# Sixteen heads' values, the state's share and the sums of squares in one block of column tiles per chunk

## What is computed

```
xn = layernorm(x)
q, k, v = silu(xn Wq'), silu(xn Wk'), xn Wv'      lf = cumsum of log_sigmoid(xn Wf' + delta) in the chunk
for each chunk, per head:
    A = (q k') * exp(lf_i - lf_j) for j <= i
    o = A v + (q exp(lf)) S
    S = exp(tot) S + (k exp(tot - lf))' v
s = (o * rsqrt(mean(o*o) + 1e-6) * norm_weight) Wo'
out = x + s * silu(experts(xn))
```

## Time and profile before

| | us |
|---|---|
| median of 3 runs | 893.77 |
| lowest and highest of them | 892.22 and 895.04 |
| the profiled execution's own time | 893.34 |
| its span in the profile | 891.6 |

### The profile page before, as it was taken

How to read it: one execution, slowest core, us unless ns; L and a number is a source line. 1 busy time by engine, 2 the same in 40 slices (tenths; PEclk the granted TensorE clock), 3 DMA queues, 4 the chain that set the end, 5 groups by cost and what they waited for, 6 DMA issues and landing times.

```text
span 891.6 us, 15824 instructions
## 1 busy us (share of the span) xinstructions
PE 800.4 (90%) x5648; PEld 682.0 (76%) x5648; DVE 566.5 (64%) x1027; ACT 498.7 (56%) x1165; POOL 429.0 (48%) x383
## 2 busy tenths in 40 slices
PE   1665799999999999999999999999999999999930
PEld 1443578888888888888888888888888888888830
DVE  5685455657855775557665766568656766556575
ACT  4654755566546664665556645665566545654431
POOL 5647641656245642566255815563357525470230
PEclk9965699999999999999999999999999999999975
DMA  8756796658667775678576766676667767663947
GB/s 284 283 166 157 206 343 221 159 152 186 194 157 159 188 195 143 150 183 202 154 160 181 156 219 142 164 187 193 157 140 193 195 157 210 162 134 117 277 106 221
DMA packets 132847, 163.89 MB, mean 184 GB/s; under 512 B 11808, under 2 KB 102432, under 8 KB 132640
## 3 DMA queue, kind: packets, MB, share of 16 engines
q1 hardware_dynamic: 119904, 145.00, 55.6%
q0 software_dynamic: 12288, 16.79, 12.1%
q10 hardware_dynamic: 576, 1.09, 0.3%
HBM read 117.48 MB, written 45.35 MB: 183 GB/s over the span
## 4 chain that ended last, share of the span: by engine, by line
PE 64%; DVE 8%; POOL 7%; ACT 5%; issue 5%; DMA 5%; SPq 1%; another core or an unknown queue 1%; DVEq 0%; ACTq 0%; POOLq 0%
PE g_ps L1408 16%; PE y_ps L1434 15%; PE up_ps L1408 15%; PE a_ps L1374 3%; PE o_ps L1398 3%; DMA qk_dram<-qk_r 3%; PE m_ps L1326 3%; PE m_ps L1356 2%; POOL w_r L803 2%; PE m_ps L1334 2%; POOL ffn_dram L833 2%; PE m_ps L1351 1%; POOL xg L821 1%; DMA w_raw<-w_experts 1%; ACT dec_both L971 1%
## 5 line engine op out<-in xcount | busy, mean ns | idle before, releaser
L1434 PE MATMUL y_ps<-w_r,hid_r 128*128 128x256 f32 x1536 | 205.5, 283 | 1.6 <-DVE hid_r L1292 1.6
L1408 PE MATMUL up_ps<-xgt,w_r 128*128 128x512 f32 x768 | 203.8, 400 | 0.0
L1408 PE MATMUL g_ps<-xgt,w_r 128*128 128x512 f32 x768 | 201.6, 398 | 1.0 <-DVE sg L1278 1.0
L1434 PEld LDWEIGHTS y_ps<-w_r,hid_r 128*128 128x128 f32 x1536 | 192.9, 190 | 3.1 <-DVE hid_r L1292 2.3
L1278 DVE SCALAR_TENSOR_TENSOR sg<-sg,g_ps 128x512 f32<-128x512 f32 x128 | 87.6, 685 | 169.2 <-ACT sg L1062 162.5
L803 POOL TENSOR_TENSOR w_r<-w_raw,w_r 128x768 fp32r<-128x768 f32 x64 | 122.3, 1912 | 101.5 <-ACT w_r L991 101.2
L1408 PEld LDWEIGHTS up_ps<-xgt,w_r 128*128 128x128 f32 x768 | 138.2, 188 | 25.9
L1408 PEld LDWEIGHTS g_ps<-xgt,w_r 128*128 128x128 f32 x768 | 135.5, 189 | 24.2 <-DVE sg L1278 0.8
L1062 ACT ACTIVATE sg<-g_ps 128x512 f32<-128x512 f32 x128 | 76.4, 597 | 125.7 <-PE g_ps L1408 121.7
L833 POOL DMA_INDIRECT ffn_dram<-y_sb,idx_all x64 | 105.0, 1640 | 74.7 <-DVE y_sb L1206 58.9
L798 POOL TENSOR_SCALAR_AFFINE_SELECT lb_row<-lb_row 128x1024 f32<-128x1024 f32 x64 | 78.2, 1232 | 95.5 <-DMA lb_row<-lb_tiles 95.4
(11 more groups left out here) (234 smaller groups left out, 950.5 us busy)
## 6 DMA issues: line engine op xcount, KB each, us to landing
lb_row<-lb_tiles SPq DMA_DIRECT2D x64, 512.0 KB, 4.5
w_raw<-w_experts SPq DMA_DIRECT2D x64, 384.0 KB
qk_dram<-qk_r SPq DMA_DIRECT2D x32, 512.0 KB, 4.4
k_st<-qk_dram SPq DMA_DIRECT2D x96, 128.0 KB, 3.3
arena<-qk_dram SPq DMA_DIRECT2D x192, 64.0 KB, 3.4
x_all<-x SPq DMA_DIRECT2D x8, 512.0 KB, 10.3
xn_dram<-xn SPq DMA_DIRECT2D x8, 512.0 KB, 5.5
e_row<-lb_tiles SPq DMA_DIRECT2D x64, 64.0 KB
```

Of the source, the lines that this page charges most:

```text
L1408: mm = pe.matmul(bank[:, :], w_r[:, m, a, at:at + P], xgt[:, b, k, half * 512:(half + 1) * 512], start=(j == 0 and k == 0), stop=(j == len ...
L1434: mm = pe.matmul(y_ps[:, j, :], hid_r[p][:, a, j * P:(j + 1) * P], w_r[:, m, b, DOWN:DOWN + D], start=(m == 0 and q == 0 and j % 2 == 0), ...
```

## The change

Every part of it is in one of three groups.

- TensorE's tiled work: `values` runs once a chunk, in the steps that are multiples of 4, and holds four things in a row: the sums of squares of the chunk before (four tiles of 32 columns, each with one moving column, into spare columns of `o_ps`), the state's share (now eight matmuls in column tiles in place of two full-width ones), and the sixteen value matmuls. The sum of squares leaves the `y` job.
- buffers: five decay buffers in place of four (the fifth shares its place with three small tables of the start), and two for the scaled keys (`kds`: `kd` and the last quarter of `k_f`). The heads lie in natural order, which changes masks and the order of weights on the host and no instruction's size.
- the tables of jobs: the three `u` jobs of a batch go from the gate place of steps 2, 7 and 13 to the down place of steps 4, 8 and 12; `kt` moves from 4 and 8 to 2 and 7, `v` of the next batch from the down place of 14 to the gate place of 13, `y` from 13 to 14. The store of `s` goes one step later on SP's queue.

```diff
-    AFTER_GATE = {0: ("kt", 0, 0), 1: ("v", 0, 1), 2: ("u", 0, 0), 3: ("x", 0, 0), 4: ("kt", 0, 1),
-                  6: ("x", 0, 1), 7: ("u", 0, 1), 8: ("kt", 0, 2), 9: ("k", 1, 0), 10: ("k", 1, 1),
-                  11: ("q", 1, 0), 12: ("q", 1, 1), 13: ("u", 0, 2), 14: ("x", 0, 2), 15: ("x", 0, 3)}
-    AFTER_DOWN = {1: ("y", -1, 3), 5: ("y", 0, 0), 9: ("y", 0, 1), 13: ("y", 0, 2), 14: ("v", 1, 0)}
+    AFTER_GATE = {0: ("kt", 0, 0), 1: ("v", 0, 1), 2: ("kt", 0, 1), 3: ("x", 0, 0), 6: ("x", 0, 1), 7: ("kt", 0, 2),
+                  9: ("k", 1, 0), 10: ("k", 1, 1), 11: ("q", 1, 0), 12: ("q", 1, 1), 13: ("v", 1, 0),
+                  14: ("x", 0, 2), 15: ("x", 0, 3)}
+    AFTER_DOWN = {1: ("y", -1, 3), 4: ("u", 0, 0), 5: ("y", 0, 0), 8: ("u", 0, 1), 9: ("y", 0, 1), 12: ("u", 0, 2),
+                  14: ("y", 0, 2)}
...
-                    if t >= 4:
-                        act.wait_ge(av_done, t // 2 - 1)
+                    if t == 4:
+                        act.wait_ge(topk, TOP_STEPS + 2)
+                    if t >= DECS:
+                        act.wait_ge(av_done, (t - DECS) // NG + 1)
...
+                def squares(ch):
+
+                    pe.wait_ge(sq_added, ch + 1)
+                    for j in range(G4):
+                        mm = pe.matmul(o_ps[PAIR * j:PAIR * (j + 1), D + ch:D + ch + 1], sq[:, 0, PAIR * j:PAIR * (j + 1)],
+                                       one_col[:, :], start=True, stop=True, skip_group_check=True)
+                    mm.then_inc(sq_summed, 1)
+
+                def values(ch):
...
+                    if ch >= 1:
+                        pe.wait_ge(o_lo, ch)
+                        squares(ch - 1)
+                    if c >= 1:
+                        pe.wait_ge(m_read, order["u", b, c - 1] + 1)
+                        pe.wait_ge(qs_done, b + 1)
+                        for k in range(KD):
+                            for j in range(G4):
+                                mm = pe.matmul(o_ps[PAIR * j:PAIR * (j + 1), k * P:(k + 1) * P],
+                                               state[:, k, PAIR * j:PAIR * (j + 1)],
                                                qs[b % 2][:, k, c * P:(c + 1) * P], start=(k == 0), stop=False,
                                                skip_group_check=True)
...
-                    if u % 2 == 0 and 2 <= u <= TS:
-                        values(u // 2 - 1)
+                    if u % NG == 0 and NG <= u <= TS:
+                        values(u // NG - 1)
```

More of the change, by code:

```diff
@@ L1304, in _ @@
                     if u == TS + 1:
-                        dve.wait_ge(m_read, order["y", B - 1, TPB - 1] + 1)
+                        dve.wait_ge(sq_summed, NT)
                         newton(0)
@@ L1355, in make @@
                             for kk in range(KD):
-                                pe.matmul(m_ps[:, 0:D], ot[:, xp, kk, :], wo_r[:, wp, kk, :], start=(j == 0 and kk == 0),
-                                          stop=(j == len(PASSES) - 1 and kk == KD - 1))
-                        pe.wait_ge(sq_added, b * TPB + m + 1)
-                        mm = pe.matmul(m_ps[:, D:D + 1], sq[:, 0, :], one_col[:, :], start=True, stop=True)
+                                mm = pe.matmul(m_ps[:, 0:D], ot[:, xp, kk, :], wo_r[:, wp, kk, :], start=(j == 0 and kk == 0),
+                                               stop=(j == len(PASSES) - 1 and kk == KD - 1))
                     elif kind == "top":
@@ L1376, in scores @@
                     mm.then_inc(a_done, 1)
-                def values(pair):
-                    ch, kk = pair // KD, pair % KD
-                    b, c = ch // TPB, ch % TPB
-                    if kk == 0:
-                        pe.wait_ge(m_read, order["v", b, c // 2] + 1)
-                        if ch >= 1:
-                            pe.wait_ge(o_lo, ch)
-                        if c >= 1:
-                            pe.wait_ge(m_read, order["u", b, c - 1] + 1)
-                            pe.wait_ge(qs_done, b + 1)
-                            for k in range(KD):
-                                mm = pe.matmul(o_ps[:, k * P:(k + 1) * P], state[:, k, :],
+                def squares(ch):
[4 more added lines that the diff above has]
+                    mm.then_inc(sq_summed, 1)
@@ L1391, in values @@
                                                qs[b % 2][:, k, c * P:(c + 1) * P], start=(k == 0), stop=False,
                                                skip_group_check=True)
[L1393 to L1400 removed]
+                        mm.then_inc(inter_done, 1)
@@ new lines, in values @@
+                    pe.wait_ge(a_read, NG * (ch + 1))
+                    for kk in range(KD):
+                        for late in range(2):
+                            for j in range(G4):
+                                h = (kk * G4 + j) * 2 + late
+                                pads = v_pad[:, c, kk * G4 + j, :, :].rearrange("p a d -> p (a d)")
+                                mm = pe.matmul(o_ps[PAIR * j:PAIR * (j + 1), kk * P:(kk + 1) * P],
+                                               pads[:, late * HD:late * HD + PAIR],
+                                               dec[(NG * ch + h // G4) % DECS][:, h % G4, :],
+                                               start=(c == 0 and kk == 0 and late == 0), stop=(late == 1),
+                                               skip_group_check=True)
@@ L1487, in _ @@
                         up(n)
-                    if u % 2 == 0 and 2 <= u <= TS:
-                        values(u // 2 - 1)
+                    if u % NG == 0 and NG <= u <= TS:
+                        values(u // NG - 1)
+                    if u == TS + 1:
+                        pe.wait_ge(o_lo, NT)
+                        squares(NT - 1)
                     if u < TS:
```

61 lines of the change are left out of this document (26 added, 35 removed).

## The result

| | before | after |
|---|---|---|
| median of 4 runs, us | 893.88 | 926.96 |
| lowest and highest | 892.22 and 895.04 | 925.38 and 927.31 |
| profiled execution, us | 893.34 | 926.83 |
| its span, us | 891.6 | 925.1 |

The changed kernel takes 1.0368 times as long, with a 95% interval from 1.0355 to 1.038. The forecast said slower, 914 us; the time lies 13 us above that, inside the range. One execution in four of experiment 4 took 1051.54 us at a mean granted clock of 0.739, where all others of this case have 0.93 to 0.96; it is left out of that experiment's figures, and why it was slow is open.

The account below looks back on a forecast made before the run. The prediction took TensorE to bound the kernel: 893.3 us plus 36 for waits at the moved `u` jobs, less 15.6 saved, gives 913.7, and the median 0.4 above: 914 us, range 894 to 936.

Parts of the forecast that it names:

- that rival's case: TensorE's clock falls behind the new waits, adding 18 to 36 us: 932 to 950 us in all, chance 0.07.
- What bounds the kernel: TensorE, busy 94.89 of a steady batch's 95.1 us, so nearly every 0.1 us on its list counts.
- The waits at steps 9 and 13: TensorE's `k` and `v` jobs wait 2.6 and 3.0 us for VectorE's late `u` read; 36 us in all.
- The 4.98 from the scores: At step 8, VectorE's next instruction after emptying `y_ps` starts 4.98 us after the scores; `advance` would stand there.
- The savings: On TensorE, one tiled block saves 0.39 us a chunk, 12.5 in all; with 3.1 from `y`'s wait, 15.6.
- up to 2 us more: Possible extra saving if the `gate` behind `y` gains from no longer following a float32 pass.
- the wait before `y`: `y` of step 13 moves to 14, no longer follows a state update: 0.45 us per batch saved, 3.1 in all.
- The rule of the Trainium skill: About 25 ns from start to start for few-column matmuls; on all eight squares passes, 0.20 us, saving 4 us less.
- The clock: In the main forecast, TensorE's clock stays at 1.00 through the loop, with nothing added to the sum.
- the lower of the two given: Cost per wait if the clock fell for one job of six matmuls: 1.4 us; with the `up` behind it, 2.8.
- The sum: Whole kernel: 893.3 + 36 - 15.6 = 913.7, with the median 0.4 above it: 914 us.

Follow-up runs that it names:

- experiment 4: Changed kernel with four and five extra matmuls ahead of the `k` job of step 9 and the `v` job of step 13, part-filling the waits: 912.13 us.
- experiment 7: Values in two tiled blocks a chunk, on top of experiment 6, against the one-block kernel of experiment 6 run beside it: 882.43 against 874.03 us.
- experiment 8: On top of Experiment 1, the sum of squares again one full-width matmul behind `y`, with ScalarE copying its result: 880.86 us.
- Experiment 1: Changed kernel, but VectorE reads the `u` job right behind its step's score in steps 4, 8 and 12, not last: 876.71 us, 0.9812 of before.
- experiment 6: On top of Experiment 1, VectorE makes the low part of `hid_r` before it splits the `k` job in step 10: 873.71 us.
- Experiment 3: Changed kernel with ten and twelve extra matmuls, results unused, ahead of the `k` and `v` jobs to keep TensorE busy in the waits: 910.46 us.
- experiment 5: On top of Experiment 1, a chunk's values in two tiled blocks again, squares and state's share ahead of the first: 882.93 us.
- experiment 2: Changed kernel with the early read of the `u` job at step 8 alone; step 12 keeps the late read: 904.73 us.

## Why the prediction was right, and where it was off

The direction, the waits and the savings came as worked out. The 914 did not: it left out the clock, and the time lies inside the range because the range reached up into that rival's case.

- **What bounds the kernel**: right. In the steady part each saving on TensorE's list showed in the time (experiments 7 and 8), and so did each wait. It did not hold at the two ends, batch 0 and the stretch behind batch 6, which the prediction had let count fully for the savings: in experiment 7 they give 0.8 us of 2.6.
- **The waits at steps 9 and 13**: right, with place, cause and size. Forecast 2.6 and 3.0 us, 5.5 per batch; measured 2.54 and 2.96, 5.5. The 4.98 from the scores to VectorE's next free place is 4.98 in the changed kernel too. Experiment 1 shows the cause: read early, and both are gone.
- **The savings**: right in kind, a little too small. Forecast 1.6 + 0.45 = 2.05 per batch, measured 2.4 (experiment 6). The squares took 0.08 (forecast 0.08), the state 0.44 (0.44), the values 0.99 (1.01). What is over lies nearly all in `gate`, which now follows `y` directly (1.37 in place of 1.46, 0.09 a chunk, 0.36 per batch), the "up to 2 us more" that the sum had left out. That the one block costs less than two is shown by experiment 7, and the worth of the squares by experiment 8; the 0.45 of the wait before `y` was not taken apart by a run. The rule of the Trainium skill weighed there (TensorE: Matmul & The Clock Gate, Back-to-back issue gap) would have made the squares 0.20; the trace does not agree for tiles side by side, eight of which take 0.08.
- **The clock**: this is the step that failed. The prediction named the mechanism, but gave it 0.07, put it at nothing in its sum and priced it for all or none: "The clock would stay at 1.00 through the loop." It fell behind ten of fourteen waits, each time for 1.55 us, 15.5 in all. It had weighed two rows, 1.48 us with no fall and 5.99 with one, and the new waits of 2.6 to 3.0 lay between. No row stood behind a chance as small as 0.07. The price of one fall, 1.4 at the lower of the two given, was nearly right. Experiment 3 shows that the low clock is a cost of its own, experiment 4 that idle time of 1.4 to 1.6 us at the same places did not bring it; what decides between equal waits stays open.
- **The sum**: 914 + 15.5 for the clock - 2.2 for the greater savings (0.37 in each of six batches) = 927.3; measured 926.96. In batches 1 to 6 alone, 6 x (5.5 - 2.05) + 14.0 - 2.2 = 32.5, and 32.3 were measured.

## What to carry to other kernels

A read-out at the end of an engine's step in an in-order list is a lock on the bank that it reads. Before moving a job, count from a common event when the writer wants the bank next and when the reader's list gets there; here that told the wait to 0.1 us, and moving the read up in VectorE's list turned 3.7% lost into 1.9% won. When waits of the size seen here are forecast for TensorE, carry the low clock behind them as a term of the sum with its own chance for each wait, not as a separate case. And after a gain on the bounding engine look for the next wait before pricing the parts: experiment 5 showed 0.20 per chunk of a true 0.33, since the kernel that it was compared with had a new wait of its own.

## What the runs showed of the hardware

- Idle time of TensorE and its clock, all at places of this loop: 1.4 to 1.6 us, no fall in twelve; 1.8 us, none in one; 2.3 us, three in six; 2.7 us, six in six in the changed kernel and four in six in experiment 2; 2.9, 3.5 and 3.9 us, once each and a fall each time. Each fall was a stretch at 0.50, and cost about 1.55 us. What decides between equal waits is open; in experiment 2 the DMA share behind a wait with a fall and one without was alike, 0.47 and 0.48.
- Entering and leaving column tiles costs TensorE time each way: at the entry 0.10 us (the state's four full-width passes take 0.54 to the first tile where their work is 0.44), at the exit 0.10 (from the scores to `down` 0.33 in place of 0.24). One more block of tiles per chunk cost 0.33 us with the work the same.
- Tiles of four column groups run side by side also when they are tiny: eight float32 passes of one column took 0.08 us.
- VectorE's subtraction of two SBUF operands, 128x512, took 4.50 us while GpSimd ran two instructions, and 0.68 without them; GpSimd's own took 2.43 and 1.67, where the same two took 1.86 and 1.09 at other places of the changed kernel (316.65 and 308.56). Both sides were slower together; which of the two held the other up was not tried.
